# Two attention layers: projections and turned shift in two row tiles that change banks, stage 0's shift rows by transfers, new orders

## What is computed

```
q = Wq x + bq            (16 x 1024)
k = Wk x + bk            (16 x 1024)
v = Wv x + bv            (128 x 1024)
attn = softmax over j of (q[:, i] . k[:, j])      (1024 x 1024)
x <- gamma * (v attn^T) + x
```

## Time and profile before

| | us |
|---|---|
| three runs, median (lowest, highest) | 198.1 (197.54, 198.36) |
| profiled execution, device time | 197.3 |
| its span | 195.5 |
| PE busy | 183.0 (94%) |
| POOL busy | 160.6 (82%) |
| ACT busy | 157.2 (80%) |
| DVE busy | 144.8 (74%) |
| TensorE clock granted | 1.00 |

### The profile page before, as it was taken

One profiled execution on the slowest core, in us unless ns is written; L12 is line 12 of the kernel. 1 busy time (PEld: TensorE's weight loads), 2 busy tenths in 40 slices (PEclk: granted clock), 3 DMA queues, 4 the chain that ended last, 5 costly groups with the idle time before them and its releaser, 6 DMA issues.

```text
span 195.5 us, 3150 instructions
## 1 busy us (share of the span) xinstructions
PE 183.0 (94%) x1117; PEld 120.8 (62%) x1119; DVE 144.8 (74%) x134; ACT 157.2 (80%) x224; POOL 160.6 (82%) x122
## 2 busy tenths in 40 slices
...
DMA packets 3869, 9.48 MB, mean 49 GB/s; under 512 B 544, under 2 KB 912, under 8 KB 3856
## 3 DMA queue, kind: packets, MB, share of 16 engines
...
...
## 4 chain that ended last, share of the span: by engine, by line
POOL 41%; PE 31%; DVE 12%; issue 9%; ACT 6%; POOLq 0%; DVEq 0%; ACTq 0%
POOL attn_lo L352 26%; PE out_psum L698 8%; POOL attn_hi L347 7%; DVE attn_lo L546 6%; PE ring L649 5%; POOL v_lo L364 5%; DVE neg_max L551 4%; PE out_psum L696 4%; ACT ring L460 4%; PE ring L625 3%; PE out_psum L732 3%; PE ring L673 3%; PE ring L635 2%; PE ring L613 2%; ACT attn L472 1%
## 5 line engine op out<-in xcount | busy, mean ns | idle before, releaser
L352 POOL TENSOR_TENSOR attn_lo<-attn,attn_hi 128x1024 fp32r<-128x1024 f32 x38 | 94.1, 2489 | 6.4 <-ACT attn_hi L478 5.8
L551 DVE TENSOR_REDUCE neg_max<-ring 128x1 f32<-128x1024 f32 x64 | 76.1, 1221 | 15.1 <-PE ring L651 14.4
L460 ACT ACTIVATE ring<-ring,neg_max 128x1024 f32<-128x1024 f32 x64 | 69.6, 1088 | 11.7 <-DVE neg_max L551 11.2
L472 ACT ACTIVATE attn<-ring 128x1024 f32<-128x1024 f32 x64 | 63.2, 1025 | 8.2 <-PE ring L675 5.6
L347 POOL TENSOR_SCALAR attn_hi<-attn 128x1024 fp32r<-128x1024 f32 x30 | 32.5, 1094 | 5.9 <-ACT attn L472 5.3
L673 PE MATMUL ring<-qk,qk_swapped 64*128 64x512 f32 x64 | 26.6, 453 | 1.2 <-ACT attn L472 0.4
L649 PE MATMUL ring<-qk_swapped,qk 64*128 64x512 f32 x56 | 25.5, 456 | 1.7 <-ACT attn L472 0.7
L675 PE MATMUL ring<-qk_swapped,qk 64*128 64x512 f32 x64 | 27.0, 459 | 0.0
L651 PE MATMUL ring<-qk,qk_swapped 64*128 64x512 f32 x56 | 25.8, 461 | 0.0
L698 PE MATMUL out_psum<-attn_hi,v_hi 64*128 64x512 f32 x72 | 22.6, 393 | 0.3 <-POOL attn_hi L347 0.3
L699 PE MATMUL out_psum<-attn_hi,v_hi 64*128 64x512 f32 x72 | 22.6, 393 | 0.0
...
## 6 DMA issues: line engine op xcount, KB each, us to landing
qk_swapped<-qk SPq DMA_DIRECT2D x16, 256.0 KB, 3.7
out_dram<-x_all SPq DMA_DIRECT2D x8, 256.0 KB, 2.0
...
x_all<-x_in SPq DMA_DIRECT2D x2, 256.0 KB, 3.0
...
qk<-shift_rows SPq DMA_DIRECT2D x7, 8.0 KB
```

What stands on the lines that cost most here:

```text
L352: nc.gpsimd.tensor_tensor(attn_lo[:, k - 1], attn[:, k], attn_hi[:, k - 1].bitcast(fp32), ALU.subtract).then_inc(cut_made["lo", "gpsimd"], 1)
L460: nc.scalar.activation(e[:], e[:], ACT.Exp, bias=neg_max[s][:, i:i + 1], accum_out=row_sum[s][:, i:i + 1]).then_inc(sum_made, 1)
L472: nc.scalar.activation(attn[:, k], ring_tile("ET", s, k)[:].rearrange("p (a n) -> p a n", a=2), ACT.Exp).then_inc(attn_made, 1)
L551: nc.vector.tensor_reduce(neg_max[s][:, i:i + 1], ring_tile("E", s, i)[:], axis=AX.X, op=ALU.max, negate=True).then_inc(max_made, 1)
```

## The change

- `project_qk` and `project_v` become two steps each, `QX` then `QK` and `VX` then `V`, with other work between them in PE's order. Step 0 multiplies array rows 0 to 63 into bank 0 and rows 64 to 127 into bank 1; step 1 does it the other way round and accumulates. Both tiles of a step write different banks. Step 1 waits by a semaphore for the end of step 0 (qk_first_mm, v_first_mm). The ring buffer belongs to the projection from step 0 on.
- `transpose_shift` uses two row tiles, 64 columns into each bank of the buffer; `rows` reads both banks by one access pattern.
- `keep_warm` makes a pair of 64-row matmuls, one per bank, where it made one with 128 rows.
- ADDED = (): stage 0's half 0 is placed by transfers as the others are (`place.0.0` in SP's order), and the eight adding matmuls of its four tiles go.
- All five orders are new. Counted by word, POOL: lo 38 to 37, hi 30 to 35, v_lo 7 to 5, v_hi 7 to 3; ACT: hi 18 to 13, v_hi 1 to 5; DVE: lo 10 to 11, v_lo 1 to 3; warm matmuls 16 to 18.

```diff
+LOWER, UPPER = slice(0, 64), slice(64, 128)
-ADDED = (0,)
+ADDED = ()
 PE_ORDER = """
-raw.0.0.0 raw.0.1.1 E.0.7.2 E.0.0.0 QK.1.0.1 E.0.3.2 E.0.2.0 V.0.0.1 E.0.1.2 E.0.4.0 E.0.6.1 warm.0.4 E.0.5.2
-warm.0.4 shift.0.0.0 E.1.6.1 E.1.7.0 warm.0.2 QK.2.0.2 ET.0.3.1 ET.0.2.0 warm.0.1 ET.0.1.1 shift.0.1.2 E.1.2.0
+raw.0.0.0 raw.0.1.1 E.0.6.2 QX.1.0.0 E.0.0.1 QK.1.0.0 E.0.7.2 warm.0.2 E.0.4.0 E.0.2.1 E.0.1.2 warm.0.2 E.0.3.0
+E.0.5.1 VX.0.0.2 warm.0.2 E.1.4.0 V.0.0.2 shift.0.0.1 warm.0.2 E.1.7.1 warm.0.2 QX.2.0.0 E.1.6.2 QK.2.0.0 warm.0.2
+ET.0.2.1 warm.0.4 ET.0.3.2 warm.0.2 E.1.5.1 ET.0.1.0 E.1.0.2 PH.0.2 E.1.2.0 PH.0.3 shift.0.1.1 E.1.3.2 ET.0.0.1
...
-PH.6.2 PV.6.1 ET.6.7.2 ET.7.0.0 ET.7.1.1 PH.6.6 PH.6.4 PV.6.3 ET.7.3.2 ET.7.2.1 ET.7.6.0 PV.6.2 PV.6.6 PV.6.7 PV.6.4
-ET.7.5.0 ET.7.4.2 ET.7.7.1 PH.7.3 PH.7.6 PH.7.1 PV.7.0 PH.7.4 PH.7.5 PV.7.1 PV.7.4 PH.7.2 PV.7.6 PV.7.2 PV.7.3
-PV.7.5 PV.7.7
+ET.6.7.1 ET.6.3.2 shift.7.1.0 PH.6.6 PH.6.4 PH.6.5 PH.6.3 PH.6.2 ET.7.3.0 ET.7.2.2 PV.6.2 PV.6.1 PV.6.3 PV.6.6
+PV.6.5 PV.6.4 ET.7.0.1 ET.7.1.0 ET.7.6.2 PV.6.7 PH.7.2 ET.7.5.1 ET.7.4.0 ET.7.7.2 PV.7.2 PH.7.3 PV.7.0 PH.7.1 PH.7.6
+PV.7.1 PV.7.3 PH.7.5 PH.7.4 PV.7.6 PV.7.5 PV.7.4 PV.7.7
 """
 ACT_ORDER = """
-sum.0.7 sum.0.0 evac.1.0 sum.0.3 sum.0.2 sum.0.1 sum.0.4 log.0.0 sum.0.6 sum.0.5 log.0.1 sum.1.6 sum.1.7 attn.0.3
+sum.0.6 evac.1.0 sum.0.0 sum.0.7 sum.0.4 sum.0.2 sum.0.1 sum.0.3 log.0.0 sum.0.5 sum.1.4 v_hi.0.0 log.0.1 sum.1.7
+sum.1.6 attn.0.2 attn.0.3 attn.0.1 sum.1.5 sum.1.0 sum.1.2 attn.0.0 sum.1.3 sum.1.1 sum.2.4 attn.0.6 log.1.1 sum.2.7
...
 SP_ORDER = """
-swap.1.0 swap.0.0 place.0.1 swap.2.0 place.1.1 swap.3.0 place.2.1 swap.4.0 place.3.1 swap.5.0 place.4.1 swap.6.0
+swap.1.0 swap.0.0 place.0.0 swap.2.0 place.0.1 place.1.1 swap.3.0 place.2.1 swap.4.0 place.3.1 swap.5.0 place.4.1
...
+        def shift_in_banks(s, h):
+            rows = P if added(s, h) else 2 * len(tiles_of(s, h))
+            return ring_tile("shift", s, h)[0:rows].rearrange("r (b q) -> r b q", b=2)[:, :, 0:64]
...
-            def project_qk(s):
+            def change_banks(step):
+                return ((LOWER, step), (UPPER, 1 - step))
+
+            def project_qk(s, step):
...
+                else:
+                    pe.wait_ge(qk_first_mm, nth_qk[s, 0])
+                for rows, h in change_banks(step):
                     part = slice(h * HALF, (h + 1) * HALF)
-                    last = nc.tensor.matmul(to[:, part], weight, x_all[:, s, part], start=True, stop=True)
-                last.then_inc(qk_mm, 1)
+                    last = nc.tensor.matmul(to[:, part], weight[rows], x_all[rows, s, part], start=step == 0, stop=step == 1)
+                last.then_inc(qk_mm if step else qk_first_mm, 1)
...
-                for j in range(TILES):
-                    last = nc.tensor.matmul(to[:, j * C:(j + 1) * C], x_all[:, s, j * P:(j + 1) * P],
-                                            late[:, WV + layer(s), :], start=True, stop=True)
+                for j in range(SLOTS):
+                    for rows, h in change_banks(step):
+                        chunk = slice((SLOTS * h + j) * P, (SLOTS * h + j + 1) * P)
+                        last = nc.tensor.matmul(to[:, chunk], x_all[rows, s, chunk], late[rows, WV + layer(s)],
+                                                start=step == 0 and j == 0, stop=step == 1 and j == SLOTS - 1)
...
-                to = ring_tile("shift", s, h)[0:P if added(s, h) else 2 * len(tiles_of(s, h)), 0:P]
-                nc.tensor.matmul(to, parts, units[:, IDENTITY], start=True, stop=True).then_inc(shift_mm, 1)
+                to = shift_in_banks(s, h)
+                for n, rows in enumerate((LOWER, UPPER)):
+                    last = nc.tensor.matmul(to[:, n], parts[rows], units[rows, IDENTITY, rows], start=True, stop=True)
+                last.then_inc(shift_mm, 1)
...
-                    nc.tensor.matmul(out_psum[:, HALF:N], zeros[:, 0:P], zeros[:], start=True, stop=True)
+                    nc.tensor.matmul(out_psum[:, 0:HALF], zeros[0:64, 0:P], zeros[0:64], start=True, stop=True)
+                    nc.tensor.matmul(out_psum[:, HALF:N], zeros[64:128, 0:P], zeros[64:128], start=True, stop=True)
```

More of the change, by code:

```diff
@@ new lines @@
+attn.1.4 attn.1.6 log.2.1 attn.1.5 attn.1.7 attn.1.0 sum.3.0 hi.1.4 v_hi.2.0 sum.3.1 sum.3.2 attn.2.3 attn.2.1
+attn.2.2 sum.3.6 sum.3.5 sum.3.4 sum.3.3 sum.3.7 attn.2.6 sum.4.4 log.3.1 attn.2.4 attn.2.5 attn.2.0 attn.2.7 hi.2.6
+sum.4.0 sum.4.7 sum.4.1 sum.4.2 attn.3.3 attn.3.0 attn.3.1 attn.3.2 attn.3.4 sum.4.5 attn.3.6 sum.4.6 attn.3.5
+hi.3.6 sum.4.3 log.4.1 sum.5.3 hi.3.5 sum.5.4 sum.5.6 sum.5.2 sum.5.1 attn.4.3 attn.4.2 attn.3.7 v_hi.4.0 attn.4.1
+sum.5.7 sum.5.5 sum.5.0 attn.4.5 log.5.1 sum.6.6 attn.4.4 attn.4.0 attn.4.6 hi.4.4 sum.6.3 hi.4.6 hi.4.5 attn.4.7
@@ L81 @@
+sum.6.2 attn.5.1 attn.5.2 attn.5.6 attn.5.3 sum.6.4 sum.6.0 sum.6.7 sum.6.5 sum.6.1 attn.5.0 log.6.1 attn.5.5
+sum.7.0 sum.7.4 sum.7.1 attn.5.4 sum.7.6 sum.7.3 attn.6.0 sum.7.2 attn.5.7 v_hi.6.0 attn.6.5 attn.6.2 sum.7.7
+attn.6.4 attn.6.1 attn.6.6 sum.7.5 log.7.1 hi.6.6 hi.6.4 attn.6.3 attn.6.7 attn.7.3 v_hi.7.0 attn.7.2 hi.7.2
+attn.7.0 attn.7.1 attn.7.6 attn.7.7 attn.7.5 attn.7.4 hi.7.5 hi.7.4
 """
 DVE_ORDER = """
-max.0.7 max.0.0 max.0.3 max.0.2 v32.0.0 max.0.1 max.0.4 max.0.6 max.0.5 rows.0.0 max.1.6 max.1.7 mask.2.0 stack.2.0
@@ L89 @@
-rows.5.1 v32.5.0 lo.4.2 max.6.6 max.6.4 max.6.7 max.6.0 finish.4.0 max.6.3 mask.7.0 max.6.5 stack.7.0 lo.5.3
-finish.4.1 rows.6.1 v32.6.0 max.7.5 max.7.0 max.7.7 lo.5.5 finish.5.0 max.7.3 max.7.1 max.7.6 max.7.2 v_lo.6.0
-max.7.4 finish.5.1 v32.7.0 rows.7.1 lo.6.3 lo.6.4 finish.6.0 finish.6.1 lo.7.1 lo.7.3 lo.7.6 lo.7.4 finish.7.0
-finish.7.1
+max.0.6 max.0.0 max.0.7 max.0.4 max.0.2 max.0.1 max.0.3 max.0.5 max.1.4 rows.0.0 v32.0.0 max.1.7 max.1.6 mask.2.0
+stack.2.0 max.1.5 max.1.0 max.1.2 rows.0.1 max.1.3 max.1.1 max.2.4 max.2.7 max.2.1 rows.1.1 v32.1.0 finish.0.0
@@ new lines @@
+max.2.3 max.2.0 mask.3.0 stack.3.0 max.2.6 max.2.2 max.2.5 finish.0.1 v32.2.0 lo.1.1 max.3.0 rows.2.1 max.3.1
+max.3.2 mask.4.0 stack.4.0 finish.1.0 max.3.6 max.3.5 max.3.4 max.3.3 max.3.7 max.4.4 finish.1.1 v32.3.0 lo.2.2
+rows.3.1 max.4.0 max.4.7 max.4.1 max.4.2 finish.2.0 mask.5.0 stack.5.0 max.4.5 max.4.6 v_lo.3.0 finish.2.1 max.4.3
+max.5.3 v32.4.0 max.5.4 rows.4.1 max.5.6 max.5.2 max.5.1 finish.3.0 mask.6.0 stack.6.0 max.5.7 max.5.5 max.5.0
+max.6.6 finish.3.1 v32.5.0 max.6.3 rows.5.1 lo.4.2 max.6.2 mask.7.0 stack.7.0 finish.4.0 max.6.4 max.6.0 max.6.7
@@ L93 @@
+max.6.5 max.6.1 finish.4.1 max.7.0 max.7.4 max.7.1 rows.6.1 max.7.6 max.7.3 finish.5.0 max.7.2 v32.6.0 lo.5.4
+max.7.7 v_lo.6.0 finish.5.1 max.7.5 v32.7.0 lo.6.5 rows.7.1 lo.6.6 lo.6.3 lo.6.4 finish.6.0 v_lo.7.0 lo.7.2
+finish.6.1 lo.7.6 lo.7.5 finish.7.0 finish.7.1
 """
 POOL_ORDER = """
-mask.1.0 stack.1.0 v_hi.0.0 parts.0.0 parts.0.1 v_lo.0.0 lo.0.2 hi.0.3 lo.0.3 hi.0.1 v_hi.1.0 hi.0.4 v_lo.1.0
-parts.1.1 lo.0.4 hi.0.5 lo.0.5 lo.0.6 hi.1.2 hi.1.3 lo.1.2 hi.1.5 hi.1.1 lo.1.1 hi.1.6 lo.1.3 parts.2.1 lo.1.6
```

106 lines of the change are left out of this document (48 added, 58 removed).

## The result

The changed kernel takes **193.1 us**, median of four runs (192.46 to 193.62), against 197.82 (197.44 to 198.36) for the kernel before on the same chip: a ratio of 0.9749 (95% interval 0.9723 to 0.9775), 4.7 us less. The forecast was 193.1 us in 189.5 to 198.8.

The account below looks back on a forecast made before the run. No engine alone: chains at the start, PE, POOL and ACT nearly full in the middle, PE at the end. Start -1.0, middle -2.4, end -1.6 gave span 190.5, execution 192.3, median 193.1 us; range 189.5 to 198.8.

Parts of the forecast that it names:

- start: Stretch up to the turned shift of stage 1 (44.5 us before), made of chains: 1.0 us less.
- middle: Stretch between the turned shifts of stages 1 and 7, 120.9 us before: 2.4 us less, to 118.5.
- end: Stretch from the turned shift of stage 7, where PE waited 2.7 us for hi and lo halves: 1.6 us less.
- Switches: PE changing between 128 rows and row tiles: 52 down to 10, 42 x 0.22 = 9.2 us less PE time.
- 174.5 us of PE by kinds: PE's stream and switches before the change, summed by kind; the listed savings and costs gave 165.5 after.
- PE throughout: Rival: PE was the bound throughout, so its 9 us pass down nearly whole: -8.6, 189.5 us; chance 0.12.
- other engines hold the pace: Rival: POOL's and ACT's middle loads don't fall, PE only idles more: middle 0, 196.6 us; chance 0.20.
- The projections themselves: QK and V on PE stream the same columns if row tiles overlap: 0 more, V at 1.71; bounds 0 and 13.7 us.
- The wait between the steps: PE's second projection step waits for the first's end, 15 times: 0.1 each, 1.5 us; bounds 0 and 4.5.
- 0.05 for the release: Estimated release part of the 0.33 us from a projection step's stream end until the next step can start.
- The orders by count: Casts counted by word in the new orders: POOL -4.5 us, ACT about -1.9, DVE +3.9.
- slower, by the start: Rival: late transfers and sums delay the first attn, deciding if after 30.0 us: +1.8, 199.9 us; chance 0.10.

Follow-up runs that it names:

- e5: Changed kernel plus one 128-row matmul of 64 columns on zeros ahead of each projection's first step: 195.45 us, 2.35 above the changed kernel.
- e12: Changed kernel with only the turned shift and the warm-up matmuls back on 128 rows, 40 switches instead of 10: 193.4 us.
- e11: Changed kernel and its orders, but each projection step is one bank on 128 rows instead of two row tiles: 200.15 us.
- e6: Changed kernel with each V step doing all four chunks of one row tile, then all of the other, instead of alternating: 199.32 us.
- e7: Changed kernel with the item between a projection's two steps moved ahead of both, so all steps are adjacent: 206.22 us.
- e2: Changed kernel with each projection whole on 128 rows at its second step's place, shift and warm-up matmuls on 128 rows: 206.06 us.
- e10: Changed kernel with each projection whole on 128 rows at its first step's place, shift and warm-up matmuls on 128 rows: 204.72 us.
- e8: Changed kernel's row-tile forms in the orders of before, ADDED = (0,), both steps of a projection directly behind one another: 200.34 us.
- e1: Changed kernel's row-tile forms in the orders of before, ADDED = (0,), a projection's steps around the item that followed it: 205.87 us.
- e13: Changed kernel's row-tile forms in the orders of before, ADDED = (0,), a projection's steps around the item that stood ahead: 206.19 us.
- e4: Changed kernel with stage 0's half 0 added in PSUM again (ADDED = (0,)) and place.0.0 out of SP's order: 193.76 us.

## Why the prediction was right, and where it wasn't

- **The time** was right: 193.1 against 193.1. That they agree to the tenth is luck, as the single terms don't. The parts by stretch were right in sign: start -1.56 (I gave -1.0), middle -1.6 (-2.4), end -1.0 (-1.6); span -4.2 (-5.0). The runs' medians then differ by 4.7, half a microsecond more than the spans.
- **Switches, 0.22 each, 42 of them, 9.2 us.** The size is roughly right at the projections: an overhead of about 0.5 fell to 0.25 in V and from 0.43 to some 0.2 in QK, 3 to 4 us over fifteen, new waits counted in. e5 has a visit at 0.28 rather than 0.44. The step that failed is the count at one price: the other 30 come to 1.2 us of PE instead of 6.6, and in the total to nothing that can be told (e12). The relief was some 4 us of PE time that matters, not 9; PE's busy time fell by 3.9. (The 174.5 us of PE by kinds that the working sets out from stands in no row; the forecast doesn't use it.)
- **How much of it arrives.** I let 2.4 us of the 9 through in the middle. e5 and e11 show shares of 0.56 and 0.71. The case "PE throughout" would have asked for a share of one and for the 30 to count; "other engines hold the pace" for a share near nothing. The measured shares lie between them, on a smaller amount; they are too rough to say nearer to which.
- **The projections themselves, 0 more.** Right, with V at 1.7, for the loop as it is written; e6 shows that the two loops exchanged cost 6.2 us.
- **The wait between the steps, 0.1 each.** Right in size (0.08). Its 0.05 for the release came from no row, but the whole of 0.33 shows in e7 as 0.34. But I priced the item between only as cover for that wait. It is what the gain rests on: moved ahead of both steps it costs 13.1 us (e7), of which the wait explains some 4. The 0.98 us that ACT idles behind a V in one block under the new orders stood nowhere in my working. The kernel before has such blocks too, but its orders covered the one at V of stage 2 to 0.17 us. This is a missing term of the sum, not one of wrong size: when ACT and DVE are served. That the idling makes up the other 9 us of e7 is argued from its rows and waits; no run gave it back alone.
- **So which part of the change made it faster?** Not one. Orders without the form: +8.5 and +6.8 against before (e2, e10). Form in the old orders: +2.4, +8.3 and +8.1 (e8, e1, e13). Together -4.7. The two row tiles make it cheap to cut a projection in two (cut on 128 rows costs 7 more, e11), and the new orders put between the halves an item that is ready and that ACT or DVE is about to need. "Switches are 9 us" got to the right total in part by luck: a term too large and a missing one offset each other.
- **The orders by count.** POOL came to 156.9 (I gave about 156), ACT fell by 1.7 (1.9). DVE rose by 0.9 instead of 3.9, mostly since its lo got shorter: 1778 ns as the mean of eleven below, from 2019.

```profile
L558 DVE TENSOR_TENSOR attn_lo<-attn,attn_hi 128x1024 fp32r<-128x1024 f32 x11 | 19.4, 1778 | 5.5 <-POOL attn_hi L359 4.7 <-ACT attn_hi L490 0.8
```

- **The start.** The second transfer of swap.1 left at 19.15, not 18.5; place.0.0 at 25.34, not 24.5; the first attn came at 29.93:

```profile
29.93 1.93 ACT L484 ACTIVATE attn<-ring 128x1024 f32<-128x1024 f32 x2
```

That is outside my 27.5 to 29.5 and 2.0 later than in the earlier trace rows: the rival "slower, by the start" was right about the late attn, and its threshold (30.0) was nearly touched. Of this 0.4 is a later start of all work (below). Of the causes that this rival named, the transfer place.0.0 isn't one: in e4, without it, the first attn comes at 29.65, nearly as late. In both kernels it stands behind sum.1.7 and sum.1.6 on ACT, which that rival named too. It didn't decide, as the other half of that step held: with two words fewer, ACT made up for it by log.1.1 (41.46, before 41.85), and shift.1.1 came at 42.94. For half 0, e4 finds no difference between transfers and selects.
- **What stays open**: the rest of the 2.4 us that e8 loses to the kernel before, and why its one late lo is so long; how much of the gain the new spread of casts brings, apart from the item between, as no run changed that alone; and whether better orders for the two-step form exist. No run here was faster than the changed kernel.
